# Second stage of a decoder block: the layer norm's reciprocal root moved to GpSimd, the rows normalised one step later, their transposes one step later still

## The reference

```python
x = x + self_attention(layernorm(x))             # 16 heads of 32, ALiBi, rational softmax
x = x + cross_attention(layernorm(x), ctx, mask) # 8 heads of 64 over 750 context rows, softmax, W_o, b_o
x = x + experts(layernorm(x))                    # router softmax, top 2 of 8, capacity 896, 512 -> 2048 -> 512
# layernorm(x) = (x - mean) / sqrt(var + 1e-5)
```

## Time and profile before

| | |
|---|---|
| median of 3 runs | 3276.03 us (3275.17 to 3278.54) |
| the profiled execution | 3286.76 us, span 3284.9 us |
| busy share of the span | PE 93%, DVE 50%, ACT 41%, POOL 22% |
| second stage, mid iterations, 860 to 1850 us | PE 951 of 990 us, DVE 572, ACT 533, POOL 200 |

### The profile page before, as it was taken

How to read it: one execution, slowest core, us unless ns; L and a number is a source line. 1 busy time by engine, 2 the same in 40 slices (tenths; PEclk the granted TensorE clock), 3 DMA queues, 4 the chain that set the end, 5 groups by cost and what they waited for, 6 DMA issues and landing times. The chain is left out here.

```text
span 3284.9 us, 50660 instructions
## 1 busy us (share of the span) xinstructions
PE 3043.6 (93%) x19312; PEld 2491.3 (76%) x19312; DVE 1644.6 (50%) x3785; ACT 1347.1 (41%) x2298; POOL 733.1 (22%) x560
## 2 busy tenths in 40 slices
PE   6889999878999999999999959999999999999997
PEld 4667777756777777777777738888888888888886
DVE  5888888863555556555555633323233323333321
ACT  5677777764555555555555521111111111121111
POOL 0000000011112122221212124242524242424232
PEclk9889999989999999999999969999999999999999
DMA  2011111124111111111111013141414141414132
GB/s 98 23 35 46 44 37 42 45 80 132 39 38 38 44 37 51 54 37 37 38 43 37 17 48 102 52 97 52 97 52 104 51 102 52 97 52 97 52 74 36
DMA packets 93874, 189.70 MB, mean 58 GB/s; under 512 B 17568, under 2 KB 27552, under 8 KB 91712
## 3 DMA queue, kind: packets, MB, share of 16 engines
q1 hardware_dynamic: 79168, 158.68, 15.9%
q0 software_dynamic: 14592, 29.43, 5.0%
HBM read 140.25 MB, written 47.82 MB: 57 GB/s over the span
## 5 line engine op out<-in xcount | busy, mean ns | idle before, releaser
L1757 ACT ACTIVATE f_hf<-f_h 128x448 f32<-128x448 f32 x256 | 139.8, 546 | 1012.4 <-PE f_h L1784 979.7
L1728 DVE CAST f_hh<-f_hf 128x448 fp32r<-128x448 f32 x256 | 106.4, 416 | 845.3 <-ACT f_hf L1757 824.5
L1799 PE MATMUL f_y<-f_w2h,f_hh 128*128 128x512 f32 x896 | 357.4, 399 | 0.0
L1687 POOL TENSOR_TENSOR f_w1l<-f_raw,f_w1h 128x512 fp32r<-128x512 f32 x128 | 182.4, 1425 | 777.3 <-DVE f_w1h L1711 777.1
L1799 PE MATMUL f_y<-f_w2h,f_hl 128*128 128x512 f32 x896 | 354.0, 395 | 0.0
L1799 PE MATMUL f_y<-f_w2l,f_hh 128*128 128x512 f32 x896 | 352.2, 393 | 0.0
L1380 ACT ACTIVATE c_s_sb<-c_s_sb,c_nmx 112x750 f32<-112x750 f32 x256 | 236.1, 922 | 200.4 <-DVE c_nmx L1214 198.5
L1372 ACT COPY c_pT<-psum 125x672 f32<-125x672 f32 x256 | 184.8, 722 | 244.8 <-PE psum L1475 236.8
L1475 PEld LDWEIGHTS psum<-a_ident,c_s_sb 112*125 112x125 f32 x1536 | 199.2, 195 | 93.7 <-issue 88.8
L1784 PE MATMUL f_h<-f_xTh,f_w1h 128*128 128x448 f32 x1024 | 254.8, 370 | 2.9 <-DVE f_xTl L1716 1.4
L1784 PE MATMUL f_h<-f_xTl,f_w1h 128*128 128x448 f32 x1024 | 250.0, 366 | 0.0
(11 more groups left out here) (246 smaller groups left out, 5833.5 us busy)
## 6 DMA issues: line engine op xcount, KB each, us to landing
f_raw<-in_w SPq DMA_DIRECT2D x128, 512.0 KB, 4.2
h_craw<-in_ctxT SPq DMA_DIRECT2D x16, 1125.0 KB, 5.1
a_x_in<-in_x SPq DMA_DIRECT2D x9, 896.0 KB, 5.7
a_xr<-in_x SPq DMA_DIRECT2D x8, 896.0 KB, 6.0
x_dram<-a_xr SPq DMA_DIRECT2D x8, 896.0 KB, 4.8
q_dram<-a_q SPq DMA_DIRECT2D x32, 224.0 KB, 5.6
h_q<-q_dram SPq DMA_DIRECT2D x16, 448.0 KB, 5.4
c_x<-x_dram SPq DMA_DIRECT2D x16, 448.0 KB, 4.9
```

The source lines that it names most:

```text
L1687: pool.tensor_tensor(w1s[1][:, l % NSLOT].rearrange("p k c -> p (k c)"), raw1[:, g % 2, l % 2, :], w1s[0][:, l % NSLOT].rearrange("p k c - ...
L1728: dve.tensor_copy(hs[0][:, l % 2, c * HC:c * HC + HC], hf[:, c, :]).then_inc(h_hi, 1)
L1757: act.activation(hf[:, c, :], H[:, 0:HC], ACT.Gelu_apprx_tanh).then_inc(free, 1)
L1799: mm = pe.matmul(Y[t][:], hs[a][:, l % 2, 128 * t:128 * t + 128], w2s[b][:, l % NSLOT, :], start=j == 0 and q == 0, stop=last_of_expert(l) ...
```

## The change

- The reciprocal root is made by POOL (`root_of_variance`, 12 instructions on 112x2 elements), in step 6 of POOL's list, when both halves' statistics (`mv_made`) are there. It uses another polynomial for the first refinement and one Newton step behind it. After each instruction POOL waits for `newton` and increments a second semaphore, `newton_seen`, by an instruction of its own.
- DVE's step 6 has no tail. In step 7, behind masking tile 9, `rows_normalised` waits for `rstd_made` and makes the two halves of `xn`.
- XT(0) moves from step 7 to step 8 behind K(1,0); XT(1) from step 8 to step 9, ahead of PV(1). The order is now K(0,0), K(0,1), K(1,0), XT(0), XT(1), PV(1). K(1,0) and XT(0) swap banks. XT(0) waits for the first half of `xn` alone, XT(1) for the second.
- ACT copies XT(0) out in step 9 behind K(1,0) and ahead of `copy_probs`, and XT(1) in step 9 behind the exponential.

```diff
-    NEWTON = 13
+    NEWTON = 12
...
-            4: ([], [OUT(1)], []), 5: ([], [PV(0)], []), 6: ([], [K(0, 0)], []), 7: ([], [K(0, 1)], [XT(0)]),
-            8: ([], [K(1, 0)], [XT(1)]), 9: ([], [PV(1)], []), 10: ([], [V(0, 0)], [RT]), 11: ([K(1, 1)], [K(2, 0)], []),
+            4: ([], [OUT(1)], []), 5: ([], [PV(0)], []), 6: ([], [K(0, 0)], []), 7: ([], [K(0, 1)], []),
+            8: ([], [K(1, 0)], [XT(0)]), 9: ([], [XT(1), PV(1)], []), 10: ([], [V(0, 0)], [RT]), 11: ([K(1, 1)], [K(2, 0)], []),
...
+        def root_of_variance(i):
+
+            var, square, product = nt[:, 0, :], nt[:, 1, :], nt[:, 2, :]
+            done = [0]
+
+            def then(ins):
+
+                done[0] += 1
+                ins.then_inc(newton, 1)
+                pool.wait_ge(newton, i * NEWTON - NEWTON + done[0])
+                pool.sem_inc(newton_seen, 1)
+
+            wait_apart(pool, mv_made, i * 2)
+            pool.sem_inc(newton_seen, 1)
+            then(pool.tensor_scalar(var, mv[:, :, 1], LN_EPS, None, ALU.add))
+            then(pool.tensor_scalar(rstd[:].bitcast(I32), var.bitcast(I32), -0.5, float(0x5f3759df), ALU.mult, ALU.add))
+            then(pool.tensor_tensor(square, rstd[:], rstd[:], ALU.mult))
...
+            then(pool.tensor_tensor(rstd[:], product, rstd[:], ALU.mult))
+            assert done[0] == NEWTON
+            pool.sem_inc(rstd_made, 1)
+
         def tail(i, kind, s):
 
+            if s == 6:
+                root_of_variance(i)
             if s == 9:
                 wait_apart(pool, xn_made, i * 2)
...
-        def layernorm(i):
...
-            dve.sem_inc(rstd_made, 1)
+        def rows_normalised(i):
             dve.wait_ge(xn_stored, i * 16 - 16)
             dve.wait_ge(rstd_made, i)
             for j in range(2):
...
-            elif s == 6:
-                layernorm(i)
+            elif s == 7:
+                rows_normalised(i)
...
+                if s == 9 and kind != "first":
+                    evacuate(i, kind, XT(0))
...
                     exponential(*step(i, s + 2))
+                if s == 9 and kind != "first":
+                    evacuate(i, kind, XT(1))
...
             elif what == "XT":
-                if m == 0:
-                    pe.wait_ge(xn_made, i * 2)
+                pe.wait_ge(xn_made, i * 2 - 1 + m)
```

More of the change, by code:

```diff
@@ L978, in projections @@
     def projections(kind, s, slots):
-        return [u for u in units(kind, s, slots) if u[0] in ("K", "V", "XT")]
+        return [u for u in units(kind, s, slots) if u[0] in ("K", "V")]
     def number(lists, i, kind, unit):
@@ L1039, in cross_attention @@
     mv_made, root_made, rstd_made, xn_made = (sem(n) for n in ("mv_made", "root_made", "rstd_made", "xn_made"))
-    newton = sem("newton")
+    newton, newton_seen = sem("newton"), sem("newton_seen")
     lg_made, le_made, route, sel_made, slots_made, sent = (sem(n) for n in ("lg_made", "le_made", "route", "sel_made", "slots_made", "sent"))
@@ L1152, in add_bias @@
             pool.tensor_tensor(x1[:], x1[:], bo[:, None, :].broadcast_to([R, 2, C]), ALU.add).then_inc(x1b_made, 1)
+        def root_of_variance(i):
[11 more added lines that the diff above has]
+            then(pool.tensor_tensor(square, rstd[:], rstd[:], ALU.mult))
+            then(pool.tensor_tensor(product, square, var, ALU.mult))
+            then(pool.tensor_scalar(square, product, -10 / 3, None, ALU.add))
+            then(pool.tensor_tensor(square, square, product, ALU.mult))
+            then(pool.tensor_scalar(square, square, 5.0, 3 / 8, ALU.add, ALU.mult))
+            then(pool.tensor_tensor(rstd[:], square, rstd[:], ALU.mult))
+            then(pool.tensor_tensor(square, rstd[:], rstd[:], ALU.mult))
+            then(pool.tensor_tensor(product, square, var, ALU.mult))
+            then(pool.tensor_scalar(product, product, -0.5, 1.5, ALU.mult, ALU.add))
+            then(pool.tensor_tensor(rstd[:], product, rstd[:], ALU.mult))
+            assert done[0] == NEWTON
+            pool.sem_inc(rstd_made, 1)
         def tail(i, kind, s):
+            if s == 6:
+                root_of_variance(i)
             if s == 9:
@@ L1383, in tail @@
         def tail(i, kind, s):
-            if kind == "end" and s in (7, 8):
-                evacuate(i, kind, XT(s - 7))
-            elif s == 11:
+            if s == 11:
                 act.wait_ge(gen_free[BANK[kind, RT]], uses_before(i, kind, RT) + 1)
@@ L1434, in _ @@
                 hi_of_outputs(B - 1, "end", NM - 1)
+            elif s == 9:
+                evacuate(B, "end", XT(0))
+                evacuate(B, "end", XT(1))
             tail(B, "end", s)
```

## The result

| | before | after |
|---|---|---|
| median, measured side by side, 20 runs each | 3274.19 us (3261.45 to 3278.54) | 3277.75 us (3273.1 to 3280.8) |
| ratio | | 1.0018 (1.0009 to 1.0026) |
| the profiled execution | 3286.76 us, span 3284.9 | 3278.75 us, span 3277.0 |

The change costs 3.6 us where 3.7 us of gain were forecast. That is less than the 0.2% that the prediction set as its bound, but the interval leaves out 1.000, so it is a small loss. Experiment 5 takes this up.

What follows compares the result with a forecast made beforehand. PE was taken to bound the second stage, busy 951 of 990 us. Mid iterations 5.6 won, clock 3.5 lost, last iteration 3.8 won, "end" 2.2 lost: 3.7 us, 3276.0 to 3272 us; 8-in-10 range 3238 to 3281.

Steps and rivals of the forecast that it cites:

- a link of the root: Root's chain on POOL: each of twelve links costs 0.30 to 0.53 us, taken as 0.38, so the root is hidden.
- L1231 takes: DVE normalising tile 9, mid iterations: POOL's addition starts first and holds it from 1317.90 to 1320.17.
- PE idle ahead of XT(1): Mid iterations: PE waits 2.2 us in one piece for ACT's copy of K(1,0), whose bank XT(1) needs.
- two places where a DVE instruction would hold the chain up: Root's chain on POOL: DVE's normalising of tiles 7 and 8 falls beside it, costing 0.41 us each at most.
- mid iterations without the clock: PV(1) starts 0.4 us earlier in each of 14 mid iterations: 5.6 us won.
- the clock in them: Mid iterations: granted clock falls as often as before, without PV(1)'s wait absorbing a part: 9 x 0.39 = 3.5 us lost.
- last iteration up to PV(1): DVE bounds it between XT(0) and PV(1); layernorm's 3.8 us leave the place ahead of tile 9: 3.8 us won.
- "end" part: From last statistics to `xn` nothing hides the root: POOL takes 5.0 us against DVE's 2.81, 2.2 us lost.
- The base: Profiled execution of before, 3286.76 us, is 10.7 us above the median 3276.03; differences from it were set against the median.
- the gap closes: Rival, chance 0.24: DVE's normalising of tile 9 isn't held, PV(1) comes up to 2.07 us earlier; 3231 to 3242 us.
- the root is dear: Rival, chance 0.10: links above 0.63 us make mid iterations lose; at 0.8 us a link, 3311 us.
- nothing moves: Rival, chance 0.06: root hidden, PE's gap merely changes place, clock falls in more iterations; 3276 to 3283 us.

Runs made afterwards that it cites:

- Experiment 5: Unchanged kernels run again on other occasions: a copy of before 3286.12 us, ratio 0.9997 to before; the changed kernel 3281.44 us, ratio 0.9985 to before.
- experiment 2: Changed kernel with five more links that change nothing in the root's chain on POOL: 3253.74 us, ratio to before 0.9903.
- third occasion: Unchanged kernels rerun on another chip: before 3273.47 us, a second copy of before 3275.07 us (1.0008), the changed kernel 3278.03 us (1.0019).
- filled after: Changed kernel with tile 8's transposes done four times, same values, ahead of XT(1): 3265.41 us (0.9936 to before); run again 3261.21 us (0.9964).
- after_again: Changed kernel, unchanged, run again beside before on a second occasion and chip: 3281.44 us, ratio to before 0.9985.

## Why the prediction was wrong, step by step

**The mechanism, in times of the iteration of the earlier trace rows.** Every step of it came out, within about 0.2 us; the measured numbers are 4.29 us later than in the fences above.

| step | forecast | measured |
|---|---|---|
| PE's wait ahead of the scores | 0.2 | 0.19 |
| a link of the root | 0.38 | 0.37 to 0.39 |
| root done | 1315.0 to 1315.8 | 1315.3 |
| `xn` ends | 1317.25 | 1317.29 |
| POOL's addition starts, takes | 1317.42, 2.35 | 1317.52, 2.38 |
| L1231 takes | 2.27 | 2.40 |
| exponential of tile 10 | 1321.25 | 1321.39 |
| PE idle ahead of XT(1) | 2.2 | 2.16 |
| PV(1) | 1323.6, 0.4 earlier | 1323.81, 0.21 earlier |

A link is 0.19 us of instruction and 0.18 to 0.20 of waiting. The prediction's two places where a DVE instruction would hold the chain up are there as well: instructions of 0.56 us (the last one, above) and 0.36 in place of 0.19, both beside an L1231. DVE's L1231 takes 2.40 us with POOL first. With DVE first by 0.12 us it takes 0.61, and POOL's addition 2.73 in place of 2.38, as experiment 2 shows. By this the rule of the exclusive lock ("SBUF — State Buffer", section "Who interferes with whom", in the Trainium skill) agrees with the traces in both directions.

**The sum.** Its terms against the differences between the third occasion's executions of before and after (a plus is time lost). The starts of PV(1) in the first and the last of the mid iterations and in the last iteration, in before and then in after:

```profile
888.46 2.49 PE L1482 MATMUL psum<-c_pT,c_v 125*64 125x224 f32 x24 [0.39 <-ACT h_kT L1368]
...
1810.97 2.49 PE L1482 MATMUL psum<-c_pT,c_v 125*64 125x224 f32 x24 [0.39 <-ACT h_kT L1368]
...
1883.79 2.49 PE L1482 MATMUL psum<-c_pT,c_v 125*64 125x224 f32 x24
```

```profile
888.01 4.01 PE L1497 MATMUL psum<-c_pT,c_v 125*64 125x224 f32 x24
...
1814.59 3.78 PE L1497 MATMUL psum<-c_pT,c_v 125*64 125x224 f32 x24
...
1884.55 2.49 PE L1497 MATMUL psum<-c_pT,c_v 125*64 125x224 f32 x24 [0.56 <-ACT c_xnT L1378]
```

| term, us | forecast | measured |
|---|---|---|
| mid iterations without the clock | -5.6 | -0.45 up to the first PV(1), then 13 x (69.83 - 70.02) = -2.5 |
| the clock in them | +3.5 | 18.8 - 12.2 = +6.6 |
| last iteration up to PV(1) | -3.8 | 69.96 - 72.82 = -2.9 |
| last iteration behind PV(1) | 0 | +2.3 |
| "end" part | +2.2 | +1.6 |
| behind the second stage | 0 | -1.2 |
| sum | -3.7 | +3.4 (spans 3269.9 and 3273.3) |

70.02 us is a period of before without a fall of the clock, filled or not. 69.83 is that of the filled after. In after itself two periods have no fall of their own, 70.13 and 70.18 us, but the next one begins in them. In before 922.51 - 13 x 70.02 = 12.2 us are left, in after 926.58 - 13 x 69.83 = 18.8. All of these are single executions.

- *The clock.* The step that failed is "I let it fall as often, now without PV(1)'s wait to absorb a part". The clock falls in 12 mid iterations instead of 10 (11 in `after_again`, 9 and 10 in the dearer executions of before). Of the 12, 11 lie within the 13 periods and cost 18.8 / 11 = 1.7 us each, instead of 12.2 / 10 = 1.2. So some 4.9 of the 6.6 us are the higher price, for which 9 x 0.39 = 3.5 were forecast, and 1.7 are one fall more. The more frequent falls were left at nothing, though the text said that the clock could fall each time. By the text's own price of 1.63 us a fall, 12 to 14 of them give 7.1 to 10.3 us lost. I took the number of falls over because the total idle time was equal, and had no row for one gap of 2.2 us in one piece.
- *The gain per iteration was half as large.* "0.4 earlier" is 0.21 (0.19 in the periods). The exponential of tile 10 came 0.14 us later than forecast: POOL started 0.23 us behind `xn` rather than 0.17, and its addition took 2.38. And PV(1) follows XT(1) on PE, 0.54 us behind XT(1)'s start at 1323.27, and not XT(0)'s copy. A term of 14 x 0.4 us can't bear errors and rounding of 0.1 us in its links. This is 2.6 us of the sum, nearly as much as the clock's 3.1.
- *The last iteration was followed only to PV(1).* In the mid iterations everything behind that mark is PE's and unchanged. In the last one DVE is the bound there. POOL's next addition, L1152, comes 5.3 us later than in before (1887.29 and 1881.99) and meets L1231 of tile 11. DVE, then POOL:

```profile
1888.74 1.31 DVE L1231 TENSOR_SCALAR c_s_sb<-c_s_sb,c_rec 112x750 f32<-112x750 f32 x1
```

```profile
1887.29 2.35 POOL L1152 TENSOR_TENSOR c_x<-c_x,c_bo 112x1024 f32<-112x1024 f32 x1 [5.71 <-DMA c_x<-x_dram]
```

  0.7 us are lost there, and PE's wait ahead of the next scores grows from 1.73 to 2.43 us. Behind those scores the same work, from tile transposes to the counts of the routing, takes 7.3 us at a granted clock of 0.60, where it took 5.3 us at 0.94 in before. But this stretch differs as much between executions of one kernel: from the last PV(1) to the last statistics it is 38.7, 38.7 and 35.2 us in the three of before (the third is the one used here) and 37.5, 38.3 and 37.5 in those of after. So only the 0.7 us are shown to be the change's.
- *The "end" part was forecast well.* From the last statistics to `xn` 5.0 us were expected. In the first profile of after it is 1931.05 - 1926.22 = 4.83, against 2.81:

```profile
1926.04 0.18 DVE L1260 BATCH_NORM_AGGREGATE c_mv<-c_stats 112x2 f32<-112x6 f32 x1
...
1931.05 1.00 DVE L1266 TENSOR_SCALAR c_xn<-c_x,c_mv,c_rstd 112x512 f32<-112x512 f32 x2 [4.83 <-POOLq L1181]
```

  0.4 us of these 2.0 don't reach the stage's end: XT(0) waits for the first half of `xn` alone now and starts 0.69 us behind the start of `xn`, where it was 1.15. The -1.2 us behind the stage lie in code that the change doesn't touch, and I have no cause for them; the three executions of before differ there by 2.9 us.
- *The base.* "It is 10.7 us above the median; I take differences from it and set them against the median" treats the difference as an offset. It was a loss of its own: some 10 us in the 13 periods beside the copy of the third occasion, with PE waits that the prediction didn't list. On an occasion of that kind the change is 4.7 us faster. That is near the forecast of 3.7 by luck, since the forecast had no term for this. On the others it is 3.6 to 4.6 us slower. That after loses less by the late start (4 us between its executions, where before loses 10) is measured; that it is the reason for the change of sign is argued.

**The rivals.** The first (the gap closes) was given its point of decision correctly, a root that ends about 1 us later, and experiment 2 shows it: 32 us below before, where the text had 34 to 45. The second (the root is dear) and its bound of 0.63 us a link were never near. The result is what the prediction called "nothing moves": the gap changes place and the clock falls in more iterations, 3276 to 3283 us. The time lies within the stated range, on the other side of no change. It shared the forecast's mechanism and got 0.06, because the forecast's clock term was set at an unchanged number of falls. What chooses between the two is one number, and the trace of before couldn't give it.

## What to carry to other kernels

When work moves from VectorE to GpSimd, follow what else the moved work releases: here an addition on GpSimd got ahead of a VectorE instruction by 0.4 us and stretched it from 0.61 to 2.40 us, and with one wait that set the order the kernel was 1.55% faster than before instead of about the same. Where TensorE's idle time only changes place, don't carry its clock losses over from the old gaps, and follow the last pass of a loop to its own bound. If the profiled execution lies 10 us above the median, look for the waits that make those 10 us before taking differences from it.

## What the hardware did that I had not expected

- Filling an idle gap of TensorE with useless matmuls made kernels faster, 16.8 us of 3278 and 7.5 us of 3273. A single wait of 2.16 us, behind an engine busy at 2.4 GHz, is followed by a granted clock of 0.50, that is 1.2 GHz, for the next 3.3 us, in 11 or 12 of 14 iterations; two waits of 1.24 and 0.91 us with 0.57 us of work between them by the same in 9 or 10. By the length of the single wait in this place, the clock fell in none of 14 iterations behind 0.39 us, in none behind 0.98, in 11 or 12 behind 2.16 and in 13 behind 2.73. Length doesn't decide alone: it fell behind each of four waits of 1.03 to 1.19 us for the copy of V in experiment 2, and behind none of the three of 1.10 us at the boundary of two iterations in before.
- A dearer chain on GpSimd (five more links, 1.9 us) made the kernel 28 us faster.
- ScalarE's first copy behind its loop's end starts 0.03 us behind what it waits for in some executions and 1.10 us in others of the same kernel. Where it starts late, a difference of 4 us between two kernels has the other sign; that the one causes the other is argued, not shown.
